# A 16-tile layer norm's statistics: x loaded ahead of the constants, first norm ahead of the weights' wait, inverse roots taken in two parts

## What is computed

```python
def _layernorm(x, axis=-1, eps=1e-05):
    m = jnp.mean(x, axis=axis, keepdims=True)
    v = jnp.var(x, axis=axis, keepdims=True)
    return (x - m) / jnp.sqrt(v + eps)

x = x + 0.5 * _L0_ffn_ref(_layernorm(x, axis=-1), ...)   # "macaron" 0: six layers of local attention
...                                                      #   and a gated feed-forward unit
```

## Time and profile before

| | before |
|---|---|
| time, median of 3 runs | 4118.94 us (4118.94, 4139.54, 4118.94) |
| the profiled execution | 4144.42 us, span 4142.6 us |
| TensorE busy (matmuls) | 3870.5 us, 93% of the span |
| VectorE busy | 3321.1 us, 80% |
| ScalarE busy | 2742.4 us, 66% |
| GpSimd busy | 2224.1 us, 54% |
| mean granted clock of TensorE | 0.953 of full speed |
| chain that ended last | PE 63%, DVE 27%, issue 6%, ACT 2% |

### The profile page before, as it was taken

How to read it: one execution, slowest core, us unless ns; L and a number is a source line. 1 busy time by engine, 2 the same in 40 slices (tenths; PEclk the granted TensorE clock), 3 DMA queues, 4 the chain that set the end, 5 groups by cost and what they waited for, 6 DMA issues and landing times.

```text
span 4142.6 us, 151779 instructions
## 1 busy us (share of the span) xinstructions
PE 3870.5 (93%) x65521; PEld 2410.0 (58%) x65521; DVE 3321.1 (80%) x6608; ACT 2742.4 (66%) x4984; POOL 2224.1 (54%) x1394
## 2 busy tenths in 40 slices
PE   6999999999999999589999999999999977999985
PEld 3666666666666666356666666666666654333333
DVE  7988888888888888588888888888888865577745
ACT  4777777777767676167777777777777742466662
POOL 4766666666666665077666666666666630000000
PEclk8999999999999999799999999999999987599996
DMA  3112121121121211012211211212111110000000
GB/s 103 41 35 57 40 57 40 40 57 40 35 57 40 57 38 43 23 29 45 51 41 40 57 40 40 57 40 57 35 43 38 35 26 0 1 1 1 1 1 11
DMA packets 138056, 154.51 MB, mean 37 GB/s; under 512 B 74392, under 2 KB 97320, under 8 KB 135728
## 3 DMA queue, kind: packets, MB, share of 16 engines
q1 hardware_dynamic: 137392, 144.81, 15.2%
HBM read 36.71 MB, written 1.05 MB: 9 GB/s over the span
## 4 chain that ended last, share of the span: by engine, by line
PE 63%; DVE 27%; issue 6%; ACT 2%; POOL 0%; DVEq 0%; SPq 0%; POOLq 0%; DMA 0%; ACTq 0%
DVE turn L666 10%; PE psum L381 10%; PE psum L449 8%; PE psum L392 8%; PE psum L417 7%; DVE nmax L724 5%; DVE den L746 5%; PE psum L441 4%; PE psum L1297 3%; PE psum L462 3%; PE psum L1285 3%; PE psum L469 3%; PE psum L479 3%; PE psum L370 2%; PE psum L1287 2%
## 5 line engine op out<-in xcount | busy, mean ns | idle before, releaser
L666 DVE TENSOR_TENSOR turn<-psum,ropes 128x512 f32<-128x512 f32 x1536 | 938.5, 672 | 31.4 <-ACT sq L554 27.1
L811 POOL TENSOR_TENSOR turn<-turn 128x1024 f32<-128x1024 f32 x384 | 904.6, 2377 | 32.6 <-DVE turn L666 32.5
L554 ACT ACTIVATE sq<-psum 128x512 f32<-128x512 f32 x768 | 451.5, 594 | 500.3 <-PE psum L370 498.9
L370 PE MATMUL psum<-wqkv,xT 128*128 128x512 f32 x1536 | 773.2, 626 | 8.5 <-DVE turn L666 6.8
L795 POOL TENSOR_TENSOR qkr<-turn,rn 128x1024 f32<-128x1024 f32 x384 | 727.9, 1918 | 17.3 <-DVE rn L687 17.2
L823 POOL TENSOR_TENSOR scratch<-scratch,rden 128x1024 f32<-128x1024 f32 x192 | 365.7, 1904 | 657.4 <-DVE rden L749 657.4
L392 PEld LDWEIGHTS psum<-ident,qkr 128*128 128x128 f32 x3072 | 329.4, 142 | 334.5 <-ACT kT L563 156.3
L392 PE MATMUL psum<-ident,qkr 128*128 128x128 f32 x3072 | 467.0, 285 | 6.7 <-POOL qkr L795 6.0
L692 DVE TENSOR_REDUCE ss<-sq 128x16 f32<-128x1024 f32 x384 | 447.9, 1207 | 0.0
L428 PEld LDWEIGHTS psum<-scratch,Vs 64*64 64x64 f32 x12288 | 330.4, 135 | 197.6 <-issue 197.2
L381 PE MATMUL psum<-wqkv,xT 128*64 128x512 f32 x1536 | 420.2, 626 | 23.2 <-DVE turn L666 6.1
(11 more groups left out here) (193 smaller groups left out, 6536.4 us busy)
## 6 DMA issues: line engine op xcount, KB each, us to landing
Vs<-V SPq DMA_DIRECT2D x384, 128.0 KB
Vs<-V SPq DMA_DIRECT2D x768, 64.0 KB
wqkv<-in_L_ffn_Wqkv_dram SPq DMA_DIRECT2D x12, 1536.0 KB
wo<-in_L_ffn_Wo_dram SPq DMA_DIRECT2D x48, 128.0 KB
zs<-Y SPq DMA_DIRECT2D x192, 31.8 KB
w<-in_L_ffn_W_dram SPq DMA_DIRECT2D x12, 341.0 KB
zs<-Y SPq DMA_DIRECT2D x168, 0.2 KB
w<-in_L_ffn_W_dram SPq DMA_DIRECT2D x12, 128.0 KB
```

Source lines behind the costliest of these rows:

```text
L370: pe.matmul(bank[b][:, :], xT[:, n // TPB % 2, bass.ts(n % TPB, P)], wqkv[n // TILES % 2][:, INNER * w:INNER * w + INNER].rearrange("p (h ...
L554: act.activation(sq[:, q // 2, q % 2, :, :], bank[QK_BANK[q]][:, :].rearrange("p (h d) -> p h d", d=RH), ACT.Square).then_inc(sem("squared ...
L666: e = dve.tensor_tensor(dst, src, tab.unsqueeze(1).broadcast_to([P, HEADS, RH]), ALU.mult)
L811: pool.tensor_tensor(t1, t1, turn2[:, w, :, :, :].rearrange("p a h d -> p (a h d)"), ALU.add).then_inc(sem("added"), 1)
```

## The change

1. x is loaded first, on a semaphore of its own (`x_loaded`), ahead of identity and rotary tables; `const_loaded` counts 17 loads.
2. On VectorE the first statistics and the first norm stand in phase 1, ahead of the wait for `const_loaded` and the copies; four of six memsets stand between the statistics and the norm. GpSimd's first roots stand ahead of the first gate.
3. The roots are taken in two parts, each with an addition and a power of its own: tiles 0 to 7 and 8 to 15 (`HALVES`), with the moments of a half right behind its statistics; behind a macaron tiles 0 to 11 and 12 to 15 (`LAST_GROUP`).
4. Inside a macaron each of the last four groups takes its four tiles' moments right behind their statistics.

The diff:

```diff
--- before.py
+++ after.py
@@ -171,7 +171,7 @@
         masks = flat(turn2[:, :, :, :, :])[:, 0:2 * NWIN]
         sel = flat(turn2[:, :, :, :, :])[0:NE, 1024:1024 + 4 * P].rearrange("p (a b) -> p a b", a=4)
         quarter = flat(turn2[:, :, :, :, :])[:, 256:256 + P]
-        LOADS = 16 * 19
+        LOADS = 16 * 17
 
         stt = sb("stt", [P, TILES, 6])
         mva = sb("mva", [P, TILES + 2, 2])
@@ -224,13 +224,12 @@
 
         def sync_program(sp):
             ld = sem("const_loaded")
+            xv = x_in.rearrange("b (s p) f -> p (b s) f", p=P)
+            sp.dma_start(X[:, 1:TPB + 1, :], xv[:, 0:TPB, :]).then_inc(sem("x_loaded"), 16)
+            sp.dma_start(X[:, TPB + 2:2 * TPB + 2, :], xv[:, TPB:, :]).then_inc(sem("x_loaded"), 16)
             sp.dma_start(ident[:, :], const[:, 0:128]).then_inc(ld, 16)
             sp.dma_start(rope[:, :, :, :].rearrange("p a t d -> p (a t d)"),
                          const[:, 384:384 + 4 * TPB * DH]).then_inc(ld, 16)
-            xv = x_in.rearrange("b (s p) f -> p (b s) f", p=P)
-            sp.dma_start(X[:, 1:TPB + 1, :], xv[:, 0:TPB, :]).then_inc(ld, 16)
-            sp.dma_start(X[:, TPB + 2:2 * TPB + 2, :], xv[:, TPB:, :]).then_inc(ld, 16)
-
             sp.dma_start(masks, maskc[:, 0:2 * NWIN]).then_inc(ld, 16)
             for i, (name, m) in enumerate((("L0_attn_W_qkv", 3), ("L0_attn_W_out", 1), ("L1_attn_w_q", 1),
                                            ("L1_attn_w_k", 1), ("L1_attn_w_v", 1), ("L1_attn_w_o", 1))):
@@ -713,6 +712,7 @@
                         dve.scalar_tensor_tensor(xs, y4, 0.5, xs, ALU.mult, ALU.add).then_inc(sem("x_updated"), 1)
                         dve.wait_ge(sem("x_updated"), 4 * c + g % 4 + 1)
                         tile_stats(dve, range(t0, t0 + 4))
+                        tile_moments(dve, STAGES.index(("macaron", c)) + 2, range(t0, t0 + 4))
 
             def step(s):
                 u, t, o, v, z = s + 2, s, s - 1, s - 3, s - 4
@@ -841,20 +841,29 @@
             for t in tiles:
                 dve.bn_stats(stt[:, t, :], X[:, slot(t), :]).then_inc(sem("x_stats"), 1)
 
-        def stats_dve(dve, n, tiles):
-            tile_stats(dve, tiles)
-            dve.wait_ge(sem("x_stats"), TILES * n)
-            for t in range(TILES):
+        HALVES, LAST_GROUP = ((0, TPB), (TPB, TILES)), ((0, TILES - 4), (TILES - 4, TILES))
+
+        def stats_dve(dve, n, parts, tiles):
+            for t0, t1 in parts:
+                tile_stats(dve, [t for t in range(t0, t1) if t in tiles])
+                tile_moments(dve, n, range(t0, t1))
+
+        def tile_moments(dve, n, tiles):
+            dve.wait_ge(sem("x_stats"), TILES * (n - 1) + tiles[-1] + 1)
+            for t in tiles:
                 dve.bn_aggr(mva[:, t, :], stt[:, t, :]).then_inc(sem("x_moments"), 1)
 
-        def stats_pool(pool, n):
-            pool.wait_ge(sem("x_moments"), TILES * n)
-            pool.tensor_tensor(rstda[:, :], mva[:, 0:TILES, 1], eps[:, :], ALU.add).then_inc(sem("x_var"), 1)
-            pool.wait_ge(sem("x_var"), n)
-            pool.tensor_tensor(rstda[:, :], rstda[:, :], half[:, 0:TILES], ALU.pow).then_inc(sem("x_rstd"), 1)
+        def stats_pool(pool, n, parts):
+            for i, (t0, t1) in enumerate(parts):
+                k = 2 * (n - 1) + i + 1
+                pool.wait_ge(sem("x_moments"), TILES * (n - 1) + t1)
+                pool.tensor_tensor(rstda[:, t0:t1], mva[:, t0:t1, 1], eps[:, t0:t1], ALU.add).then_inc(sem("x_var"), 1)
+                pool.wait_ge(sem("x_var"), k)
+                pool.tensor_tensor(rstda[:, t0:t1], rstda[:, t0:t1], half[:, t0:t1], ALU.pow).then_inc(
+                    sem("x_rstd"), 1)
 
         def norm_dve(dve, n):
-            dve.wait_ge(sem("x_rstd"), n)
+            dve.wait_ge(sem("x_rstd"), 2 * n)
             for t in range(TILES):
                 dve.tensor_scalar(Y[:, t, :], X[:, slot(t), :], mva[:, t, 0:1], rstda[:, t:t + 1], ALU.subtract,
                                   ALU.mult)
@@ -1536,12 +1545,15 @@
 
         @block.vector
         def _(dve):
+            dve.memset(eps[:, :], LN_EPS)
+            dve.memset(half[:, :], -0.5)
+            dve.wait_ge(sem("x_loaded"), 32)
+            stats_dve(dve, 1, HALVES, range(TILES))
             dve.memset(xT[:, :, :], 0.0)
             dve.memset(ss[:, :], 1.0)
             dve.memset(gT[:, 2, :], 1.0)
-            dve.memset(half[:, :], -0.5)
-            dve.memset(eps[:, :], LN_EPS)
             dve.memset(ones[:, :], 1.0)
+            norm_dve(dve, 1)
             dve.wait_ge(sem("const_loaded"), LOADS)
             dve.tensor_copy(identb[:, :], ident[:, :])
             dve.tensor_copy(selb[:, :, :], sel[:, :, :])
@@ -1554,9 +1566,11 @@
                 if i and not in_macaron:
                     dve.drain().then_inc(sem("stage_done"), 1)
                     dve.wait_ge(sem("stage_done"), sum(k != "macaron" for k, _ in STAGES[0:i]))
-                stats_dve(dve, i + 1, () if in_macaron else range(TILES))
-                if kind == "macaron":
-                    norm_dve(dve, i + 1)
+                if i:
+                    if not in_macaron:
+                        stats_dve(dve, i + 1, HALVES, range(TILES))
+                    if kind == "macaron":
+                        norm_dve(dve, i + 1)
                 finish_phase_dve(dve, i + 2)
                 if kind == "macaron":
                     macaron_dve(dve, c)
@@ -1570,9 +1584,11 @@
 
         @block.gpsimd
         def _(pool):
+            stats_pool(pool, 1, HALVES)
             finish_phase(pool, 1)
             for i, (kind, c) in enumerate(STAGES):
-                stats_pool(pool, i + 1)
+                if i:
+                    stats_pool(pool, i + 1, LAST_GROUP if STAGES[i - 1][0] == "macaron" else HALVES)
                 finish_phase(pool, i + 2)
                 if kind == "macaron":
                     macaron_pool(pool, c)
```

## The result

| | before | after |
|---|---|---|
| median, measured side by side, 8 runs each | 4132.86 us (4117.27 to 4140.34) | 4102.32 us (4081.82 to 4110.23) |
| ratio, 95% interval | | 0.9938 (0.9914 to 0.9962) |
| the profiled execution, its span | 4144.42, 4142.6 | 4095.8, 4094.0 |
| TensorE busy | 3870.5, 93% | 3834.8, 94% |
| VectorE busy | 3321.1, 80% | 3322.2, 81% |

By that ratio the change is faster by 0.62% (25.6 us; the interval is 16 to 36); the two medians in the table lie 30.5 us apart. A second series gave 0.9946 (0.9919 to 0.9974). The forecast was 4098.0 with a range of 4082 to 4124; its gain of 20.9 us lies inside the interval.

A forecast was written before the change was run, and what follows sets the result against it. The prediction read the seams as the bound, where other engines wait at the gate, since TensorE's busy time is nearly all untouched macarons. -11.1 - 3.8 - 6.0 = -20.9 us off the 4118.9 median gave 4098.0, range 4082 to 4124.

The forecast's parts named there:

- Step 1, the start: Program start: statistics, roots and first norm go beside the loads, L370 starts at 21.5 instead of 32.62; -11.1 us.
- The clock at the start: Start, TensorE's granted clock: half speed before, TensorE still idles there, so nothing was counted; 0 us.
- Step 2, the halves: Seams into macaron 1, the attention and the last experts: power over 8 columns 1.55 us, gain 1.25 each; -3.8 us.
- Rival (a): GpSimd's power does not get shorter with fewer columns; gain only 10.6 us, 4108; chance 0.04.
- Step 3, behind the macarons: Behind both macarons: gate passes 3.1 us after last group's statistics, -4.0 each, -3.0 after cost of moments; -6.0 us total.
- moments in the tail: Macaron's last groups: moments on VectorE delay its run into L724; cost 0.4 to 1.2 us per macaron, taken as 1.0.
- The median taken off: Whole kernel: gain subtracted from the runs' median, 4118.9 us, not the profiled 4144.4; 4098.0.
- The signs: Wrong if 8-column power exceeds 2 us, first macaron matmul after 23, or attention's first two sections off 144 by over 21.
- (b): Three seams: first half's power holds VectorE's second-half statistics, each loses 1.8 us and gains 1.25; -15.4 in all, 4103.5; chance 0.05.
- (c): Start: weights or x land late, so the start gives 3 to 6 us less; 4101 to 4104; chance 0.04.
- (d): Whole kernel: the clock gives more (about 4085, chance 0.15) or takes some back (4119, chance 0.15).
- (e): Attention, slower: clock comes back only after the second section, 4138 us, or after the third, 4160; chance 0.06.

The follow-up runs named there:

- the combined kernel: Changed kernel with six scale transfers issued from ScalarE's queue at program start, wqkv ahead of Wo, norm waiting per root half; 4102.21 us, 0.9939 of the kernel before.
- the start alone: Kernel before with only the changed start (x first, statistics and norm early), whole roots, no moments in the tail; 4115.9 us, 0.9981 of the kernel before.

## Why the prediction was right, and where it wasn't

**Step 1, the start (-11.1): -8.3.** VectorE's side held in kind, but "x is there by 6 us at the latest" did not: the second half was issued 0.9 us earlier, not 1.4, x's packets moved for 4.0 us (1.8 to about 5.9), not 3.0, and the statistics began at 6.85. So the norm ended at 18.2 instead of 17.3, the copies at 19.0 instead of 18.2, and the gate passed at 19.8 instead of 19.5. None of it was paid for, because the next thing was later still. The step that failed is "that gap is where they have landed, and I take 21.5", with its bound of 22.5: they land at 24.3. A dip in the DMA share was read as an end, and it was a slow part, in the trace of before as well (scales up to 23.7). The price is 2.8 us.

**The clock at the start (0): about -2.5.** The last issue of layer 0 that SyncE makes in step with the tiles (wqkv of the layer after next) went from 334.84 to 323.97, -10.9, of which -8.3 is the first product. I had set the clock at nothing because TensorE idles here. It still fell, but came back 10 us earlier, with TensorE's work. In the second trace of the changed kernel the issue stands at 325.25 and the first product at 24.45, so there this term is -1.4; of the kernel before there is one trace. So two errors of opposite sign made the start's sum look right.

**Step 2, the halves (-1.25 each, -3.8): -1.24, -1.22 and -1.18, -3.6.** A power of 8 columns takes 1.64 where I had put 1.55. Rival (a) is out: 0.39 + 0.158 per column, where I had 0.2 + 0.17.

**Step 3, behind the macarons (-4.0 each): -3.92 and -3.91.** Of the moments in the tail only the first of three distances is shown, +0.41 in both macarons. By the two traces the other two changed by +0.35 and +0.16 in macaron 1, but by -0.32 and -0.49 in macaron 0, less than they vary by themselves. So the 1.0 that I put for each macaron is neither shown nor refuted, and the sum of -6.0 lies in the -5.4 to -7.0 that costs of 1.2 and 0.4 leave.

**The sum** by landmarks is -8.3 - 3.6 - 6.0 = -17.9 (-17.3 to -18.9 by the bounds of step 3), and with the clock of the start -20.4; the forecast was -20.9. The fit at equal clock gives 13.2 ± 1.8, to be set beside the 17.9; with the 3.7 us of low clock cut out of the start it is 16.9, beside the 20.4. Both fall short, by 4.7 and 3.5 us. The late records of the clock may account for a part; the rest stays open.

**The median taken off.** The three runs shown have a median of 4118.9, the 56 of the later series a mean of 4128.9. The forecast's base was 10 us low, and it left out the 8 us by which the rest of the clock was better. The two nearly cancel, so that 4098.0 stands so close to 4102.3 is in part luck.

**The signs.** Of the three that the prediction named for its being wrong, one did not show (a power over 8 columns takes 1.64, under 2) and two did: the first product with wqkv started at 24.3, after 23, and the attention's first two sections took 122.0 us together, 22.3 less than before, where 21 was the limit. The start's end and the clock are where the mechanism was off.

**The rivals.** (b), GpSimd holding VectorE, is out: statistics beside a power took 1.61 against 1.64, and the norm beside one is not held either (16 tiles in 4.33 us, 4.19 without). By the rule quoted from the Trainium skill (SBUF — State Buffer, "SBUF: two separate sides") an operation of VectorE with two SBUF inputs would be held by one of GpSimd's that reads SBUF, as the power does; the Newton steps L673 and L676 have two, stand beside the power at 1678.68, and take 0.20 each, as everywhere. Here rule and trace differ, and the trace decides: a power held nobody. The plainest case is L772 itself, which starts in the middle of the changed kernel's power over 12 columns and takes its usual 0.18:

```profile
1663.72 2.28 POOL L862 TENSOR_TENSOR rstda<-rstda,half 128x12 f32<-128x12 f32 x1
```

```profile
1664.38 0.18 DVE L772 TENSOR_SCALAR rn<-ss 128x33 int32<-128x33 int32 x1 [1.27 <-ACT zn L601]
```

L772 was held by L805 again elsewhere (0.72 at 1741.74 in the kernel with the norm on halves), but not at 19.88 (0.18), where L805 came later. (c), weights late, held in kind: 2.8 us less, just below its 3 to 6. (d), the clock giving more, is what the means and the fit show, by about 8 us. (e), low clock past the attention's second section, is not in the changed kernel's profile; the combined kernel's profile comes close to it (84.8 and 72.8, then 57.9), at 4140.9 us where (e) put 4138.

## What to carry to other kernels

Before taking an "it has landed" from a gap in DMA traffic, look for small transfers in the queue: a few rows of 128 to 256 bytes, repeated over 128 partitions, made such a gap here and held what stood behind them. The sizes of the packets tell them apart. Ask whether an engine waits for transfers that it does not read (here TensorE for the scales; to part them was not tried). Read the granted clock only where its record has begun, and check it by the length of a known instruction. Split a step in two only where the first part finds cover; where both parts stand in the open the split costs its fixed part. Where the clock's share of the time (here 3.1 us for each 0.001) is larger than the effect, compare kernels at equal mean clock, and single edits by landmarks in the trace.

## What the runs showed of the hardware that was not expected

- Six transfers of 16 to 32 KB, each a row of 128 or 256 bytes to all 128 partitions, ran at 13 GB/s and a DMA share of 0.07 for some 4 us, and cost 4 to 5 us on either queue.
- GpSimd's power costs 0.39 us + 0.158 us per column of 128 rows, an addition 0.20 to 0.22 whatever the size; it held no operation of VectorE beside it, whereas GpSimd's multiplication over 128x256 (L805) made VectorE's L772 take 0.71 instead of 0.18.
- The same instructions, the attention's first section, took from 58.5 to 84.8 us over 14 profiles, at mean granted clocks from 0.87 down to 0.50. Fifteen extra products ran at 2.4 GHz; the clock fell 5 us behind them.
- In every trace here the first products with wqkv ran at half clock. With the start alone the column of the clock reads 1.00 up to 32 us, yet weight loads took 0.34 us up to 28.2, as at 0.50 elsewhere: there the column says nothing of the clock.
